# A decoder layer on one core: the expert input's rounding and its low part in two pieces of 512 columns in place of one of 1024

## The reference, cut to what matters

```python
def expert(muW, gW, gqa, gqb, gs, uW, uqa, uqb, us, dW, dqa, dqb, ds, w):
    xe = x + w @ muW.T
    gate = jax.nn.silu(_fused_linear(xe, gW, gqa, gqb, gs, w))
    up = _fused_linear(xe, uW, uqa, uqb, us, w)
    return _fused_linear(gate * up, dW, dqa, dqb, ds, w)
```

## Time and profile before

| | |
|---|---|
| median of 3 runs | 999.36 us |
| lowest and highest | 998.17 and 1001.8 us |
| the profiled execution's own time | 1000.12 us |
| its span, first to last instruction | 998.5 us |
| TensorE matmul busy | 906.4 us, 91% |
| VectorE busy | 667.7 us, 67% |
| ScalarE busy | 518.9 us, 52% |
| GpSimd busy | 376.8 us, 38% |
| granted TensorE clock, mean | 0.962 of full speed |

### The profile page before, as it was taken

How to read it: one execution, slowest core, us unless ns; L and a number is a source line. 1 busy time by engine, 2 the same in 40 slices (tenths; PEclk the granted TensorE clock), 3 DMA queues, 4 the chain that set the end, 5 groups by cost and what they waited for, 6 DMA issues and landing times. The chain is left out here.

```text
span 998.5 us, 15713 instructions
## 1 busy us (share of the span) xinstructions
PE 906.4 (91%) x5588; PEld 791.6 (79%) x5588; DVE 667.7 (67%) x1315; ACT 518.9 (52%) x1218; POOL 376.8 (38%) x252
## 2 busy tenths in 40 slices
PE   6899999999999997878698978999999999999993
PEld 5799999999999995757577856878787878787882
DVE  4756465565556564657569758777777777778775
ACT  4555574655665553234343436556565556565543
POOL 1721231212221211326215227464656565656420
PEclk9899999999999998889788989999999999999996
DMA  6300000000000001200010112020202020200002
GB/s 222 97 1 22 1 21 11 11 11 11 11 11 11 0 12 49 81 1 1 1 61 8 69 48 74 31 81 24 82 22 83 22 81 21 81 21 22 22 1 85
DMA packets 16428, 37.97 MB, mean 38 GB/s; under 512 B 2048, under 2 KB 6912, under 8 KB 15232
## 3 DMA queue, kind: packets, MB, share of 16 engines
q1 hardware_dynamic: 15744, 35.29, 10.5%
q0 software_dynamic: 640, 2.10, 0.7%
HBM read 34.76 MB, written 2.62 MB: 37 GB/s over the span
## 5 line engine op out<-in xcount | busy, mean ns | idle before, releaser
L234 POOL TENSOR_TENSOR att_probs<-att_probs,att_share 128x512 f32<-128x512 f32 x64 | 66.4, 1039 | 192.1 <-DVE att_share L517 192.1
L1459 POOL TENSOR_TENSOR all_xT_hi<-moe_xe,all_xT_hi 128x1024 fp32r<-128x1024 f32 x31 | 80.7, 2603 | 99.5 <-ACT all_xT_hi L1598 98.6
L421 ACT ACTIVATE att_probs<-att_score,att_bias 128x128 f32<-128x128 f32 x256 | 90.7, 380 | 42.1 <-DVE att_bias L508 41.9
L1467 POOL TENSOR_TENSOR all_xT_lo<-moe_inner,all_xT_lo 128x512 fp32r<-128x512 f32 x64 | 84.3, 1317 | 72.4 <-ACT all_xT_lo L1637 69.0
L1637 ACT ACTIVATE all_xT_lo<-moe_inner 128x512 fp32r<-128x512 f32 x64 | 40.3, 630 | 92.5 <-DVE moe_inner L1707 92.5
L1707 DVE TENSOR_TENSOR moe_inner<-moe_gu,moe_silu 128x512 f32<-128x512 f32 x64 | 43.9, 686 | 62.3 <-ACT moe_silu L1633 58.8
L554 DVE SCALAR_TENSOR_TENSOR att_OT_lo<-att_mix,att_bv,att_OT_hi 128x512 fp32r<-128x512 f32 x64 | 45.9, 750 | 58.8 <-ACT att_OT_hi L459 58.8
L459 ACT ACTIVATE att_OT_hi<-att_mix,att_bv 128x512 fp32r<-128x512 f32 x64 | 43.6, 704 | 66.6 <-PE att_mix L50 66.5
L48 PE MATMUL att_proj<-att_xT_hi,att_Wq_hi 128*128 128x256 f32 x256 | 74.8, 292 | 1.3 <-DVE att_Wq_lo L482 0.5
L48 PE MATMUL att_acc<-att_Wo_hi,att_OT_hi 128*128 128x256 f32 x256 | 73.0, 285 | 1.6 <-DVE att_OT_lo L554 1.6
L295 PEld LDWEIGHTS att_score<-att_KT,att_QT 128*128 128x128 f32 x512 | 63.2, 198 | 12.0 <-issue 9.1
(11 more groups left out here) (298 smaller groups left out, 2923.1 us busy)
## 6 DMA issues: line engine op xcount, KB each, us to landing
all_stage<-in_expert_w SPq DMA_DIRECT2D x8, 1152.0 KB, 5.5
moe_spread<-soft_dram SPq DMA_DIRECT2D x64, 128.0 KB
all_scale<-in_expert_scale SPq DMA_DIRECT2D x8, 320.0 KB, 5.9
att_xT<-in_xT SPq DMA_DIRECT2D x8, 256.0 KB, 3.1
att_stage<-in_Wq SPq DMA_DIRECT2D x4, 512.0 KB, 7.3
att_stage<-in_Wo SPq DMA_DIRECT2D x4, 512.0 KB, 6.2
att_x_tok<-in_x_tok POOLq DMA_DIRECT2D x8, 256.0 KB, 3.1
out<-all_r SPq DMA_DIRECT2D x4, 512.0 KB, 4.4
```

The source lines that it names most:

```text
L234: pool.tensor_tensor(p3, p3, each, ALU.mult).then_inc(prob_ready, 1)
L421: ins = act.activation(p_[:, c], score[b][:, c], ACT.Exp, bias=bias[b][:, h:h + 1], scale=SCALE, accum_out=m_[:, h:h + 1])
L1459: pool.tensor_tensor(xe[u % 2].lo[:, :], xe32[:, :], xe[u % 2].hi[:, :].bitcast(F32), ALU.subtract).then_inc(xe_lo, 1)
L1467: pool.tensor_tensor(innerT[u % 2].lo[at], inner[at], innerT[u % 2].hi[at].bitcast(F32), ALU.subtract).then_inc(inner_lo, 1)
```

## The change

ScalarE's rounding of `xe32` and GpSimd's subtraction become two instructions each, one for each half of 512 columns. ScalarE's first one waits for the first half of the sum only, and GpSimd's first one for ScalarE's first one. The semaphores `xe_hi` and `xe_lo` count two for each unit; TensorE and VectorE wait for both. The same is done to the first unit's low part on VectorE.

```diff
             def xe_low(g, u):
 
-                pool.wait_ge(xe_hi, count(g, u + 1))
-                pool.tensor_tensor(xe[u % 2].lo[:, :], xe32[:, :], xe[u % 2].hi[:, :].bitcast(F32), ALU.subtract
-                                   ).then_inc(xe_lo, 1)
+                for k in range(DK):
+                    at = slice(k * CT, (k + 1) * CT)
+                    pool.wait_ge(xe_hi, 2 * count(g, u) + k + 1)
+                    pool.tensor_tensor(xe[u % 2].lo[:, at], xe32[:, at], xe[u % 2].hi[:, at].bitcast(F32), ALU.subtract
+                                       ).then_inc(xe_lo, 1)
...
-                        pe.wait_ge(xe_lo, count(g, u + 2))
+                        pe.wait_ge(xe_lo, 2 * count(g, u + 2))
...
             def xe_high(g, u):
-                act.wait_ge(xe32_ready, 2 * count(g, u + 1))
-                act.activation(xe[u % 2].hi[:, :], xe32[:, :], ACT.Copy).then_inc(xe_hi, 1)
+                for k in range(DK):
+                    at = slice(k * CT, (k + 1) * CT)
+                    act.wait_ge(xe32_ready, 2 * count(g, u) + k + 1)
+                    act.activation(xe[u % 2].hi[:, at], xe32[:, at], ACT.Copy).then_inc(xe_hi, 1)
...
             xe_sum(0, 0)
-            dve.wait_ge(xe_hi, 1)
-            dve.tensor_tensor(xe[0].lo[:, :], xe32[:, :], xe[0].hi[:, :].bitcast(F32), ALU.subtract).then_inc(xe_lo, 1)
-            dve.wait_ge(xe_lo, 1)
+            for k in range(DK):
+                at = slice(k * CT, (k + 1) * CT)
+                dve.wait_ge(xe_hi, k + 1)
+                dve.tensor_tensor(xe[0].lo[:, at], xe32[:, at], xe[0].hi[:, at].bitcast(F32), ALU.subtract
+                                  ).then_inc(xe_lo, 1)
+            dve.wait_ge(xe_lo, 2)
             xe_sum(0, 1)
...
-                        dve.wait_ge(xe_lo, count(g, u + 2))
+                        dve.wait_ge(xe_lo, 2 * count(g, u + 2))
                         xe_sum(g, u + 2)
```

More of the change, by code:

```diff
@@ L1584, in _ @@
             inputs(0, 1, 0)
-            pe.wait_ge(xe_lo, 1)
+            pe.wait_ge(xe_lo, 2)
             low_rank(0, 0, 0)
```

## The result

The changed kernel takes 1013.12 us (median of 4 runs, 1010.63 to 1014.11) against 998.76 us before (4 runs beside it). The ratio is 1.0137, 95% interval 1.0110 to 1.0163: slower, where I had forecast 995.9 us and at most 1004.5. Its profiled execution has a span of 1012.5 us, 14.0 more than before. Lines have moved: L1598 is now L1602, L1459 L1461, L1682 L1686, L1685 L1689, L1717 L1721, L1765 L1772, L1502 L1504, L1690 L1694, L1707 L1711, L1467 L1469; the weight split is still L1037. The list of VectorE's order above leaves one instruction out: in the second unit of each turn the copy of the shares (L1765, now L1772) stands between the added output and the first gate product.

What follows compares the result with a forecast made beforehand. TensorE was taken to set the pace of most units, with a stall every four units; -0.97 - 7.7 + 0.9 + 4.3 = -3.5 us gave 995.9 us, range 991.5 to 1004.5.

Steps and rivals of the forecast that it cites:

- the part on ScalarE: ScalarE's added rounding instruction: 0.13 us in each of 7 units that round weights, +0.9 us, at most +2.2; elsewhere hidden.
- W: The 7 units in which weights are rounded and split; only ScalarE's extra instruction was to cost there, 0.13 us each.
- P: The 7 units after a weight-splitting one: L1685 waits for one GpSimd half only, 1.10 us gained each, -7.7 us.
- S: The 16 other units: GpSimd's half starts just before L1685 and delays it, +0.32 or +0.22 us each, +4.3 us.
- The start: First unit, low part on VectorE in halves: its second subtraction ends sooner, -0.97 us.
- the first rival: VectorE wins the close start against GpSimd in S, which then costs nothing: 991.6 to 993.3 us, chance 0.22.
- The second rival: In P GpSimd gets ahead of the first L1682, so the gain is lost: 1005.8 us, chance 0.18.
- The third: A waiting VectorE instruction isn't let in between GpSimd's halves, so L1685 waits for both: about 1033 us, chance 0.04.

Runs made afterwards that it cites:

- e4: The kernel before, with only the copy of the shares moved from VectorE to ScalarE: 998.45 us, ratio 0.9994.
- e1: The changed kernel with the copy of the shares moved from VectorE to ScalarE: 994.78 us, ratio 0.9962 to the kernel before.
- e7: The kernel before, no halves, with the copy of the shares one place later on VectorE, behind the first gate product: 1007.72 us, ratio 1.0092.
- e8: The changed kernel with the copy on ScalarE and pieces of 256 and 768 columns on ScalarE and GpSimd: 990.42 us, ratio 0.9913 to the kernel before.
- e3: The kernel before with ScalarE's rounding alone in two halves, GpSimd subtracting 1024 columns in one: 998.67 us, ratio 1.0000.
- e2: The kernel before with GpSimd's subtraction alone in two halves, ScalarE rounding 1024 columns in one: 992.51 us, ratio 0.9934.
- e5: The kernel before with GpSimd's subtraction alone in pieces of 256 and 768 columns, ScalarE whole, copy on VectorE: 987.42 us, ratio 0.9888.
- e10: The changed kernel with pieces of 256 and 768 columns on ScalarE and GpSimd, copy left on VectorE: 999.80 us, ratio 0.9996 to the kernel before.

## Why the prediction was wrong

**The step that failed** is the last sentence of the part on ScalarE: "L1685's delay by the first half in W is covered, because L1707 waits for that L1633." As time the delay was covered, and e4 shows that the copy between them costs nothing while it comes first. But the copy L1765, whose row I had read the earlier trace rows and used only to show who gets in between two GpSimd instructions, is itself held by GpSimd, and L1037 is up half a microsecond behind it. A delay of 1.09 us in front of it, taken as zero, moved it across. In its place the runs showed:

- the held copy: the three W are 14.3 us longer in the changed kernel than in e1 (4.76, 4.77 and 4.73);
- what goes with it: the three P behind them lack the gain that they have in e1 (-1.10 to -1.11 each), 3.5 us. TensorE has idled 5.0 us; the granted clock is 0.53 from 708 to 714 us, and 20 of the 24 output matmuls go at 0.21 us and not 0.12, 1.9 us more. e7 shows the same with a shorter idle stretch.

The chain of the changed kernel at that place:

```profile
709.51 0.21 PE moe_y L48
...
713.57 0.21 PE moe_y L49
...
713.92 0.12 PE moe_y L48
...
714.27 0.23 PE moe_gu L48
```

In this P GpSimd has had over 4 us more to catch up, and the pair's second instruction is no longer held. The first row is of the P at 660 us, behind a copy that isn't held, the second of this one:

```profile
658.69 2.40 DVE L1686 TENSOR_TENSOR moe_low_pair<-moe_low,moe_low_pair 64x512 fp32r<-64x512 f32 x2
...
711.89 1.40 DVE L1686 TENSOR_TENSOR moe_low_pair<-moe_low,moe_low_pair 64x512 fp32r<-64x512 f32 x2
```

So VectorE is held in this P only as in an S, and an S takes 11.83 us; yet the P takes 13.83, about as long as before. My estimate is that nearly all of the 2.0 us between them is the clock's; no run shows a held copy at full clock.

14.3 + 3.5 = 17.8 us, of 17.5 between the two kernels by their ratios and 18.3 by their times.

**The other terms** stood in the main, as e1 shows, which has them all without the held copy. Forecast -3.5 us by the sum; e1 is 3.8 us below the kernel before by its ratio of 0.9962, 2.3 to 5.4 by the interval. Its trace's units add up to -5.0.
- P: -7.7 forecast, -7.9 in e1 (seven of -1.10 to -1.18). That VectorE gets in between the halves was right in every P.
- S: +4.3 forecast, +3.9 in e1 (15 units; the sixteenth has no next rounding to measure to). GpSimd won the close start each time: the first rival, that VectorE wins it (0.22), falls. It was closer than I had it in some turns: GpSimd led by 0.02 to 0.03 us in the first and the last and by 0.09 in the two between, where 0.07 was forecast. That L1685 is "already through" when L1459 starts in the kernel before was misread: L1459 starts 0.40 us behind L1685's start and 0.29 before its end. It needed only to be first. e8 shows the cause by size: with the first piece halved, S costs nothing.
- ScalarE: +0.9 forecast, +0.2 in e3. The term was too large twice: the second instruction takes 0.09 us and not 0.13 (the weight rounding starts 1.04 us behind the first half, before it was 0.95), and though the gate product is 0.09 to 0.10 later in all seven W, only two of them are that much longer at the next rounding.
- The start: -0.97 forecast, -1.19 by the trace of the changed kernel, -1.36 in e1, -0.81 in e3 where only ScalarE's part is in halves.

**The second rival**, the loss of P's gain on the slow side, did not come in the changed kernel by its own mechanism: the pair L1686 keeps its order with L1469 there. The third didn't either: in e2 and in the changed kernel the low part takes 1.68 us in P, a hold by one half. All my cases looked at L1682 and L1685, and none at the copy. What would have shown it was in the trace of the kernel before, one query beyond the rows that I had taken: list each VectorE instruction that GpSimd can hold in W (L1682, L1685, L1765, L1695), move each by the delay just worked out, and look what is up on GpSimd then. The one with 0.53 us to the 5.16 us instruction was the risk.

**The three longer S in e2** (and in e5) are one more hold. GpSimd's weight scaling lies in these units, its L1469 comes later behind it, and VectorE's L1697 (L1695 before, the low part of the down projection's low-rank product) waits for it. In the unit that takes 11.99 us for 11.56 the row of before and the two of e2 are:

```profile
694.68 1.15 DVE L1695 TENSOR_TENSOR all_xT_lo<-moe_dlow,all_xT_lo 64x512 fp32r<-64x512 f32 x1 [0.70 <-ACT all_xT_lo L1608]
```

```profile
690.72 2.73 POOL L1469 TENSOR_TENSOR all_xT_lo<-moe_inner,all_xT_lo 128x512 fp32r<-128x512 f32 x2 [0.56 <-POOL all_stage L1032]
...
692.40 1.59 DVE L1697 TENSOR_TENSOR all_xT_lo<-moe_dlow,all_xT_lo 64x512 fp32r<-64x512 f32 x1 [0.70 <-ACT all_xT_lo L1610]
```

L1697 is 0.44 us longer and the unit 0.44; in the other two it is 0.24 and 0.10 longer than its counterpart before, and the units 0.24 and 0.09. Why GpSimd idles 0.56 us behind the scaling there stays open.

## What to carry to other kernels

Where two engines hold each other up, what counts is which one is up first: after any change in time list the held pairs again, the short ones too, and look for the long instruction just behind a short one. Splitting the holder's instruction is a gain where the other engine is already waiting, and a loss where it lets the holder start first; here the same halves on GpSimd gave 0.9934 with the start kept and 1.0137 with it moved (0.9962 with the copy out of the way). A fragile order can be taken off the shared path: in this kernel 0.26 us on ScalarE bought 18 us.

## What the runs showed of the hardware that I had not expected

- The start decides within less than 0.1 us: 0.03 us behind is 5.15 us, 0.08 us ahead is 0.19 us (e10). In S a lead of 0.02 to 0.09 us was enough for GpSimd, in all 15 such units of the changed kernel.
- A copy of 32 columns is held as long as what is left of the holder's instruction, and is through 0.05 us behind its end; a low part of 512 columns 0.55 us behind it. So the row of the held instruction tells where the holder ended.
- TensorE's clock fell after idling 2.7 to 3.2 us in all four turns of e7, in one of them with 1.3 us of its own work at full pace in between, and the output matmuls at the 1.2 GHz level ate most of what the next unit would have given back.
